# A two-layer graph network on one core: a front stage written out tile by tile, and a constants' product and a new order in the attention gather

## The reference

```python
xn = _layernorm(x, axis=-1)
x = x + _L1_gnn_ref(xn, edge_index, W, a, Wo, bo) + _L1_mix_ref(xn[None], Wq, Wkv, Wproj, bproj)[0]
x = x + _L1_ffn_ref(_layernorm(x, axis=-1)[None], ...)[0]
# _L1_gnn_ref, 8 heads of 64:
h = jnp.einsum('ni,hio->nho', x, W)
e = s_src[src] + s_tgt[tgt]                      # s = <h, a> by head
e = jnp.where(e >= 0, e, NEG_SLOPE * e)
ex = jnp.exp(e - m[tgt])                         # m: a bound of e by target
out = segment_sum(h[src] * (ex / denom[tgt]), tgt) @ Wo + bo
# _L1_mix_ref, linear attention: q, k = elu + 1
context = einsum('bhnd,bhne->bhde', k, v);  attn = q @ context * D_inv
```

## Time and profile before

| | us |
|---|---|
| three runs | 2878.69, 2885.69, 2886.76 |
| median | 2885.69 |
| the profiled execution, its own time | 2852.97 |
| its span, first to last instruction | 2850.8 |
| front1, from its first instruction to the barrier | 1425 to about 1602 |
| attend | about 1606 to 2256 |

### The profile page before, as it was taken

The page is one execution under the profiler, slowest core; times in us unless marked ns, Lnnn a source line. Parts: engine busy times, 40 slices in busy tenths (PEclk is TensorE's granted clock), DMA queues, the critical chain, the costliest instruction groups (busy, mean ns, idle before and its releaser), DMA issues. The chain is left out here.

```text
span 2850.8 us, 33290 instructions
## 1 busy us (share of the span) xinstructions
PE 2189.6 (77%) x9696; PEld 1390.9 (49%) x9696; DVE 1522.6 (53%) x3022; ACT 700.8 (25%) x1795; POOL 851.5 (30%) x879
## 2 busy tenths in 40 slices
PE   0299996888888885699668466777766685999998
PEld 0065653333343445566435255555555574555555
DVE  6977665666767652433254466666666682111111
ACT  0011111111111112133123243434333132222322
POOL 2000003656565630255300355555555100000000
PEclk9999997999999996699889789999888895999999
DMA  1111112323232356133310466666666302000001
GB/s 43 35 74 59 74 59 80 87 73 87 81 89 83 89 60 209 23 60 57 74 50 37 123 171 175 176 177 187 169 180 175 69 8 83 1 0 0 0 1 36
DMA packets 112634, 236.00 MB, mean 83 GB/s; under 512 B 22425, under 2 KB 66860, under 8 KB 109801
## 3 DMA queue, kind: packets, MB, share of 16 engines
q0 software_dynamic: 56784, 160.68, 22.2%
q1 hardware_dynamic: 55704, 73.57, 7.6%
HBM read 193.62 MB, written 40.57 MB: 82 GB/s over the span
## 5 line engine op out<-in xcount | busy, mean ns | idle before, releaser
L2182 PE MATMUL p_ag<-rows_g,oh_g 128*128 128x260 f32 x1488 | 439.9, 438 | 196.7 <-DVE rows_g L2096 103.8
L608 POOL DMA_INDIRECT rows<-h_table,row_rel x372 | 357.7, 962 | 659.1 <-SPq L531 438.9
L2051 POOL DMA_INDIRECT rows_g<-g_table,row_src x372 | 351.8, 946 | 467.0 <-POOLq L95 195.2
L2182 PEld LDWEIGHTS p_ag<-rows_g,oh_g 128*128 128x128 f32 x1488 | 279.0, 208 | 232.6 <-issue 183.1
L860 PE MATMUL p_agg<-rows,oh 128*128 128x256 f32 x744 | 204.0, 408 | 36.0 <-DVE x L659 26.2
L2473 DVE SCALAR_TENSOR_TENSOR x<-p_yf,cw,x 128x256 f32<-128x256 f32 (+1 forms) x160 | 66.3, 477 | 306.4 <-PE p_yf L2564 306.4
L2079 DVE TENSOR_TENSOR acc<-acc,p_ag 128x520 f32 x186 | 128.7, 692 | 168.8 <-PE p_ag L2182 101.1
L2096 DVE TENSOR_TENSOR rows_g<-rows_g,p_n 128x2048 f32<-128x2048 f32 x93 | 212.0, 2279 | 0.0
L860 PEld LDWEIGHTS p_agg<-rows,oh 128*128 128x128 f32 x744 | 134.8, 195 | 106.0 <-issue 50.0
L728 DVE TENSOR_TENSOR fT<-a_sb,p_sel 128x512 f32<-128x512 f32 x200 | 129.0, 684 | 102.8 <-PE p_sel L908 47.7
L2564 PE MATMUL p_yf<-f,h_f 128*128 128x256 f32 (+1 forms) x640 | 145.3, 380 | 0.8 <-ACT h_f L2505 0.8
(11 more groups left out here) (433 smaller groups left out, 3381.1 us busy)
## 6 DMA issues: line engine op xcount, KB each, us to landing
h_table<-h_out SPq DMA_DIRECT2D x20, 1024.0 KB
where_g<-d_table SPq DMA_DIRECT2D x93, 128.0 KB
w<-in_L_ffn_W SPq DMA_DIRECT2D x16, 512.0 KB, 9.5
rows<-h_table,row_rel POOLq DMA_INDIRECT x372
rows_g<-g_table,row_src POOLq DMA_INDIRECT x372
g_table<-row SPq DMA_DIRECT2D x20, 260.0 KB
f<-in_L_ffn_W SPq DMA_DIRECT2D x16, 256.0 KB
x_acc<-x SPq DMA_DIRECT2D x1, 2560.0 KB
```

The costliest lines, as they stand in the source:

```text
L608: pool.indirect_dma_start(rows[:, r, j], None, st.h_rows, bass.IndirectOffsetOnAxis(ap=st.row_rel[:, at:at + 1], axis=0)).then_inc(gathere ...
L2051: pool.indirect_dma_start(rows[:, r, j], None, st.g_table, bass.IndirectOffsetOnAxis(ap=st.row_src[:, at:at + 1], axis=0)).then_inc(gather ...
L2182: last = pe.matmul(p_a[:, k % 2, h, 0:HALF], oh[:, r, j], rows[:, r, j, h * HALF:(h + 1) * HALF], start=j % SUP == 0, stop=j % SUP == SUP - 1)
```

## The change

In front1 the loops are written out on all engines with constant indices, two semaphore sets of the loop (`held`, `row_free`) go, and the order changes. TensorE turns tile t + 1 between the scores and the context product, the context product of a tile comes one tile later, and TensorE waits for `w_a` only before the first score product. VectorE starts with `rstd` and two `norm`s before it sums `w_a`, takes the minima of a tile, norms tile t + 2, makes the features and adds the context of the tile before. The storing of rows is waited for by the tile that uses the place again.

GpSimd clears `acc` in front1; in attend VectorE no longer does. In attend VectorE issues `weigh(s)` ahead of both `add_sum`s of batch s - 1. TensorE issues ahead of its waits for `oh` and `weigh(s)`, for s = 1 to 89, one product of two constants, the identity and three copies of `iota` (384 columns), into columns 128 to 511 of a `p_n` bank; nothing reads them.

```diff
@@ front1, sync
-            sp.sem_inc(row_free, 2)
-            with sp.Fori(0, T // 2) as i:
-                for u in range(2):
-                    t = 2 * i + u
-                    hold(sp, h_copied, t + 2, held)
-                    hold(sp, s_taken, t + 1, held)
-                    sp.dma_start(st.g_table[ds(t * P, P), :], row[:, u]).then_inc(row_stored, 16)
-                    sp.wait_ge(row_stored, (t + 1) * 16)
-                    sp.sem_inc(row_free, 1)
+            for t in range(T):
+                sp.wait_ge(h_copied, t + 1)
+                sp.wait_ge(s_taken, t + 1)
+                sp.dma_start(st.g_table[t * P:(t + 1) * P, :], row[:, t % 2]).then_inc(row_stored[t % 2], 16)
+        @block.gpsimd
+        def _(pool):
+            pool.memset(st.acc[:, :], 0.0).then_inc(acc_cleared, 1)
+            pool.wait_ge(acc_cleared, 1)
@@ front1, vector
+            norm(0)
+            norm(1)
...
+            for t in range(T):
+                take(t)
+                if t + 2 < T:
+                    norm(t + 2)
+                features(t)
+                if t:
+                    add_context(t - 1)
+            add_context(T - 1)
@@ front1, scalar
+            take_x(0)
+            for t in range(T):
+                if t + 1 < T:
+                    take_x(t + 1)
+                act.wait_ge(neg_ready, t + 1)
+                nc.scalar.activation(neg[:, t % 2], neg[:, t % 2], ACT.Exp).then_inc(exp_ready, 1)
+                act.wait_ge(h_ready, t + 1)
+                if t >= 2:
+                    act.wait_ge(row_stored[t % 2], 16 * (t // 2))
+                nc.scalar.copy(row[:, t % 2, 0:HF], p_h[:, :]).then_inc(h_copied, 1)
@@ front1, tensor
-            pe.wait_ge(wa_ready, 1)
...
+            turn(0)
+            for t in range(T):
+                pe.wait_ge(xT_ready, t + 1)
...                                                  (p_kv, then p_q by w_q)
+                if t == 0:
+                    pe.wait_ge(wa_ready, 1)
...                                                  (p_q by w_a)
+                if t + 1 < T:
+                    turn(t + 1)
+                if t:
+                    context_product(t - 1)
+                if t:
+                    pe.wait_ge(h_copied, t)
...                                                  (p_h)
+            context_product(T - 1)
@@ attend, vector
-            link(dve.memset(st.acc[:, :], 0.0))
...
-                if s:
-                    add_sum(GR * (s - 1), tiles[0])
                 weigh(s)
                 if s:
-                    add_sum(GR * (s - 1) + 1, tiles[1])
+                    for g in range(GR):
+                        add_sum(GR * (s - 1) + g, tiles[g])
                 tiles = tiles_of(s)
@@ attend, tensor
             for s in range(NBATCH):
                 r = s % RING
+                if 0 < s < NBATCH - 3:
+                    pe.matmul(p_n[:, (s + 3) % NR, P:], st.ident[:, :], st.iota[:, :].unsqueeze(1).broadcast_to([P, 3, P]),
+                              start=True, stop=True, skip_group_check=True)
                 pe.wait_ge(oh_ready, s + 1)
                 pe.wait_ge(msg_ready, s + 1)
```

More of the change, by code:

```diff
@@ L1655, in front1 @@
         w_in = sem("w_in1")
-        held = sem("held1")
         dv = sem("dv_front1")
@@ L1674, in front1 @@
         c_used = sem("c_used1")
-        row_stored = sem("row_stored1")
-        row_free = sem("row_free1")
+        row_stored = [sem(f"row_stored{u}") for u in range(2)]
         ends_ready = sem("ends_ready1")
@@ L1684, in front1 @@
         place_turned = sem("place_turned1")
+        acc_cleared = sem("acc_cleared1")
         place_ready = sem("place_ready1")
@@ L1717, in _, with norm, take @@
             dve.sem_inc(var_ready, 1)
+            dve.wait_ge(sd_ready, 1)
+            link(dve.reciprocal(rstd[:, :], sd[:, :]))
+            def norm(t):
+                if t >= 2:
+                    dve.wait_ge(transposed, t - 1)
+                dve.tensor_scalar(xn[:, t % 2], st.x[:, t * D:(t + 1) * D], mean[:, t:t + 1], rstd[:, t:t + 1],
+                                  ALU.subtract, ALU.mult).then_inc(xn_ready, 1)
+            def take(t):
+                u = t % 2
+                dve.wait_ge(kv_ready, t + 1)
+                if t:
+                    dve.wait_ge(exp_ready, t)
+                dve.tensor_scalar(neg[:, u, 0:D], p_kv[:, 0:D], 0.0, None, ALU.min)
+                link.inc(dve.tensor_scalar(v_m[:, u, 0:D], p_kv[:, D:], live[:, t:t + 1], None, ALU.mult))
+                link.inc(dve.tensor_copy(v_m[:, u, D:D + 1], live[:, t:t + 1]))
+                dve.wait_ge(q_ready, t + 1)
+                dve.tensor_scalar(neg[:, u, D:], p_q[:, 0:D], 0.0, None, ALU.min).then_inc(neg_ready, 1)
+                if t >= 2:
+                    dve.wait_ge(row_stored[u], 16 * (t // 2))
+                dve.tensor_copy(row[:, u, HF:], p_q[:, D:D + H])
+                dve.tensor_copy(st.s_all[:, t * 2 * H:(t + 1) * 2 * H], p_q[:, D:D + 2 * H]).then_inc(s_taken, 1)
@@ new lines, in features @@
+            def features(t):
+                u = t % 2
+                dve.wait_ge(exp_ready, t + 1)
+                dve.scalar_tensor_tensor(out=k_f[:, u], in0=p_kv[:, 0:D], scalar=0.0, in1=neg[:, u, 0:D],
+                                         op0=ALU.max, op1=ALU.add).then_inc(kv_used, 1)
+                dve.scalar_tensor_tensor(out=st.qT[:, t * D:(t + 1) * D], in0=p_q[:, 0:D], scalar=0.0, in1=neg[:, u, D:],
+                                         op0=ALU.max, op1=ALU.add).then_inc(q_used, 1)
@@ L1721, in _ @@
+            link(dve.tensor_copy(live[:, T - 1:T], st.rowmask[:, :]))
+            link(dve.memset(context[:, :, :], 0.0))
+            link(dve.memset(st.cb[:, :, :], 0.0))
+            link(dve.memset(ones[:, :], 1.0))
             dve.wait_ge(w_in, 64)
@@ L1729, in _ @@
             dve.sem_inc(wa_ready, 1)
[L1730 to L1783, removed]
@@ L1826, in _, with take_x @@
             nc.scalar.activation(sd[:, :], sd[:, :], ACT.Sqrt).then_inc(sd_ready, 1)
[L1827 to L1842, removed]
+            def take_x(t):
+                act.wait_ge(transposed, t + 1)
+                if t >= 2:
+                    act.wait_ge(h_ready, t - 1)
+                nc.scalar.copy(xT[:, t % 2], p_t[:, t % 2, 0:D]).then_inc(xT_ready, 1)
+            take_x(0)
[5 more added lines that the diff above has]
+                act.wait_ge(h_ready, t + 1)
+                if t >= 2:
+                    act.wait_ge(row_stored[t % 2], 16 * (t // 2))
+                nc.scalar.copy(row[:, t % 2, 0:HF], p_h[:, :]).then_inc(h_copied, 1)
             act.wait_ge(z_asked, 1)
@@ L1852, in _, with turn @@
             pe.wait_ge(w_in, 64)
-            pe.wait_ge(wa_ready, 1)
             pe.wait_ge(place_ready, 1)
-            pe.sem_inc(transposed, 2)
-            def context_product(t, u):
+            def turn(t):
+                pe.wait_ge(xn_ready, t + 1)
+                if t >= 2:
+                    pe.wait_ge(xT_ready, t - 1)
+                for k in range(K):
+                    last = pe.transpose(p_t[:, t % 2, k * P:(k + 1) * P], xn[:, t % 2, k * P:(k + 1) * P], st.ident[:, :])
+                last.then_inc(transposed, 1)
@@ L1859, in context_product @@
+            def context_product(t):
                 pe.wait_ge(kv_used, t + 1)
-                pe.wait_ge(c_used, t + 1)
+                if t:
+                    pe.wait_ge(c_used, t)
                 for c in range(2):
-                    last = pe.matmul(p_c[:, c, 0:D + 1], k_f[:, 1 - u, c * P:(c + 1) * P], v_m[:, 1 - u], start=True, stop=True)
+                    last = pe.matmul(p_c[:, c, 0:D + 1], k_f[:, t % 2, c * P:(c + 1) * P], v_m[:, t % 2], start=True, stop=True)
                 last.then_inc(c_ready, 1)
[L1866 to L1871, removed]
-                    for k in range(K):
[L1873 to L1894, removed]
@@ L1895, in _ @@
-            context_product(T, T % 2)
+            turn(0)
+            for t in range(T):
+                pe.wait_ge(xT_ready, t + 1)
+                halves = [xT[:, t % 2, k * P:(k + 1) * P] for k in range(K)]
+                if t:
+                    pe.wait_ge(kv_used, t)
+                for k in range(K):
+                    last = pe.matmul(p_kv[:, :], halves[k], w_kv[:, k], start=k == 0, stop=k == K - 1)
+                last.then_inc(kv_ready, 1)
+                if t:
+                    pe.wait_ge(q_used, t)
+                for c in range(2):
+                    for k in range(K):
+                        pe.matmul(p_q[:, c * P:(c + 1) * P], w_q[:, k, c * P:(c + 1) * P], halves[k], start=k == 0, stop=k == K - 1)
+                if t == 0:
+                    pe.wait_ge(wa_ready, 1)
+                for k in range(K):
+                    last = pe.matmul(p_q[:, D:D + 2 * H], halves[k], w_a[:, k], start=k == 0, stop=k == K - 1)
+                last.then_inc(q_ready, 1)
+                if t + 1 < T:
+                    turn(t + 1)
```

(7 more changed lines are left out.)

10 lines of the change are left out of this document (8 added, 2 removed).

## The result

| | before | changed |
|---|---|---|
| four runs each, us | 2885.69, 2878.69, 2886.76, 2880.16 | 2787.20, 2795.59, 2792.78, 2800.36 |
| median | 2882.93 | 2794.19 |
| profiled execution, own time (span) | 2852.97 (2850.8) | 2787.20 (2784.6) |

The ratio is 0.969, 95% interval 0.966 to 0.972: 89 us less. The forecast was 2802 us, 84 less.

A forecast was written before the change was run, and what follows sets the result against it. front1 was taken as bound by TensorE, attend by a chain through several engines with TensorE's news often late. Terms -25 - 3 - 56 = -84 from the profiled 2853 gave 2769, plus 33 to the median: 2802 us, range 2738 to 2870.

The forecast's parts named there:

- front1, -25: front1: written-out, reordered tiles cost 6.0 us without `p_kv` waiting, and an earlier start saves 4.8; -25 us, bounds -15 and -30.
- Clearing of acc, -3: Clearing moved to idle GpSimd in front1 lets attend's first scores come up to 6 us sooner; -3 us, bounds 0 and -6.
- New order, -56: attend: early `weigh` cuts late batches to 7.0 us, with no slow batch behind; others 5.43; -56 us.
- The constants' product, 0: attend: holds the clock through TensorE's gap, but the order alone should do that; 0 us gain.
- No cost of the product: attend: TensorE's batch of 4.2 us plus 0.7 stays below 5.43, so 0; up to +62 us if uncovered.
- How often news are late: attend: TensorE's completion signals arrive late in two batches of five, 36 at 7.0 us and 55 at 5.43.
- Rival B: Only front1 gains; TensorE's products really end when their news arrive, so attend's constants' product costs 62 us; 2864 us, chance 0.2.
- Rival C: attend: late and slow batches alternate, the clock still falling in the gap, mean interval 7.45 us; 2929 us, chance 0.1.

The follow-up runs named there:

- x1: The changed kernel without the constants' product in attend, front1 and the new order kept; 2809.05 us, ratio 0.974 to the kernel before.
- x4: The changed kernel with the constants' product issued twice in a row; 2783.84 us, ratio 0.966 to the kernel before.
- first set: Four kernels that take the change in attend apart, on one chip where the kernel before took 2882.92 us.
- x5: The changed kernel with attend's 372 indirect gathers replaced by plain transfers issued by SP, GpSimd idle in attend; 2861.11 us (kernel before 2661.75).
- x7: The changed kernel with GpSimd issuing a batch's gathers two by two, each pair behind one half's sum; 2632.92 us (kernel before 2661.75).
- fourth set: The unchanged kernel before, profiled on another chip; 2661.43 us.

## Why the prediction was right, and where it was not

- **front1, -25**: measured -28.8. The mechanism holds: `p_kv` waits nowhere, of the ten table loads in the tiles one is left, a tile costs 5.8 us where 6.0 was reckoned (18 tiles 104.7, forecast 108), and the start saved 5.0 (from the first statistics to the second tile's `p_kv` 29.6 us before, 24.5 now), forecast 4.8.
- **Clearing of acc, -3**: -0.7 in the profiled pair, since the next two `scores` still wait for late news there, 9.26 us and 11.88 us. On chips without late news it is the -5.2 above, near the bound of -6.
- **New order, -56**: right in direction, too large as the order's own share: -42 in attend's intervals, -47 timed. The failed step is that with the order TensorE "idles about 2 us instead of 5.11, so no slow batch follows". The prediction's own numbers give this only with the product in them: a late interval of 7.0 less a batch of 4.9 us is 2.1, but less the batch of 4.2 that the order alone has it is 2.8. Without the product (x1) the gaps are 2.77 to 3.25 us, 21 of 22 are followed by slower passes (2.07 us for four instead of 1.12), and the clock in attend is 0.89, no better than before.
- **The constants' product, 0**: "the order alone should do that, so it gets no gain of its own" is the same failed step from its other side. It gives 23 us in attend's intervals (571.9 to 548.6). That the total of attend came out (-58.6 against -56) is luck: two misses of opposite sign. The clock was forecast to be 1.00 throughout and was 0.98.
- **No cost of the product**: right. On a chip without late news one is hidden in VectorE's round (487.5 us with it, 486.6 without). On the late chip even two cost nothing (x4), in intervals whose mean is 6.0 us; two were not tried on a chip without late news.
- **How often news are late**: forecast two batches in five at 7.0 and the rest at 5.43. Measured: 14 at about 7, but 48 of the others near 6.0 or 6.5. The mean, 6.03, agrees with 6.05 for a reason the forecast didn't have: most batches are a little late. A reading of the late batch's rows, not tested: if the news of the second half come about 2 us late, the chain is weigh, TensorE's batch, late news, second addition, scores, hot and the weigh two batches on.
- **Rival B**, only front1 gains: its time (2864) and its price of 62 us for the product fall, for attend gained 58.6 and doubling the constants' product on the late chip lost nothing. Its mechanism, products that really end when their news arrive, was not measured, since the ends are modelled. Against it stand the starts: in the late batch of the earlier trace rows the four groups start within 3.11 us as in a quick one, so TensorE itself was not held up between them. Rival C, 2929, needed a clock that falls with the product too; it stays at 0.98.

What makes the news late is open. It goes with the chip: every profile of the first set has it, as do the two of the result, and none of the other three sets has it, with one chip in each; what differs between these chips was not looked for. That GpSimd's issues have a part in it rests on the rows before alone, since both experiments on it (x5, x7) ran on chips without late news. The issues by themselves do not bring it about: on those chips GpSimd issues four gathers in every 5.3 us, more densely than on the late one. Whether the product must stand ahead of the waits on a chip with late news wasn't tried there either.

## What to carry to other kernels

Where an engine's news come late, put other work ahead of the instruction that waits and ask for the news later; here this costs some 5 us on a chip without such lateness and saves 42 on one with it. A filler on TensorE is worth its place only in gaps that bring the clock down, and only if what is left of the gap is short enough: look at the duration of the same passes behind each gap (2.07 against 1.12 us) before adding one, count the gaps again with it, and then try it doubled. Do one change at a time in the trace even when the sum fits: here the sum was right and two of its terms were not.

## What was not expected of the hardware

The same kernel differs by 8% between chips (2883 against 2662 to 2665 us), with the same duration of the instructions compared (`weigh` 2.28 us, an issue of a gather 0.95 us, on both). The two profiles of the kernel before are 195 us apart (spans 2850.8 and 2655.8), and nearly all of it lies in the stages that gather with GpSimd: 607 against 482 us in attend's intervals, 40 against 29 at its start, and 59 us in layer 0, the time up to front1's first statistics (1425.2 against 1366.4 us), where the page's row of the gathers shows the idle time, first of the kernel before as profiled at the start, then in the fourth set:

```profile
L608 POOL DMA_INDIRECT rows<-h_table,row_rel x372 | 357.7, 962 | 659.1 <-SPq L531 438.9
```
```profile
L608 POOL DMA_INDIRECT rows<-h_table,row_rel x372 | 361.3, 971 | 595.7 <-SPq L531 439.8
```

A gain measured on one chip (89 us) can be a third of that on another (29 us): it is well to compare within one chip and to say what the kernel before took there.
